# The last layer of a two-layer network on one core: values read in their PSUM bank, a projection step of their own, and another order of the turn

## What is computed

```python
# first attention: within one token, 16 heads of 16
Q, K, V = (x @ W.T).reshape(B, L, H, hd) for each of W_Q, W_K, W_V
sK = softmax(swapaxes(K, -1, -2), axis=-1)
tran_V = einsum('bldh,blhe->blde', sK, V)
x = layernorm(x + einsum('blhd,blde->blhe', softmax(Q, axis=-1), tran_V))
# second attention: layernorm, queries against 64 context rows under a mask, projection
x = layernorm(x + cross_attention(x, ctx, ...))
# feed-forward with ternary weights
h = silu(lin(x, w1)) * lin(x, w2)
h = gelu(lin(h, h1)); h = gelu(lin(h, h2))
x = layernorm(x + lin(h, w3))
```

## Time and profile before

| | |
|---|---|
| median of 3 runs | 1357.84 us (1355.26 to 1358.79) |
| profiled execution | 1360.66 us, its span from the first to the last instruction 1359.0 us |
| mean granted clock in the span | 0.908 |
| TensorE busy | 1072.8 us, 79% of the span |
| VectorE busy | 936.5 us, 69% |
| ScalarE busy | 592.4 us, 44% |
| GpSimd busy | 363.3 us, 27% |
| last layer | about 660 us to the end of the span |

### The profile page before, as it was taken

The page is one execution under the profiler, slowest core; times in us unless marked ns, Lnnn a source line. Parts: engine busy times, 40 slices in busy tenths (PEclk is TensorE's granted clock), DMA queues, the critical chain, the costliest instruction groups (busy, mean ns, idle before and its releaser), DMA issues. The chain is left out here.

```text
span 1359.0 us, 21042 instructions
## 1 busy us (share of the span) xinstructions
PE 1072.8 (79%) x6769; PEld 893.7 (66%) x6770; DVE 936.5 (69%) x1865; ACT 592.4 (44%) x1626; POOL 363.3 (27%) x493
## 2 busy tenths in 40 slices
PE   1599999675787599999425688888888888887887
PEld 1378888552376388889213577776777768776787
DVE  5689999766773012222399998989899898989321
ACT  0244444140361323323002466757665655757553
POOL 1001011100033200000500344626363443636232
PEclk9789999885895699999666799999999999999899
DMA  8015710000006656665270000000000000000000
GB/s 285 16 70 183 248 35 5 1 0 0 1 1 249 254 206 224 240 246 197 66 312 0 1 1 1 8 0 8 0 0 8 0 8 0 8 0 8 1 9 9
DMA packets 23974, 98.88 MB, mean 73 GB/s; under 512 B 3728, under 2 KB 15184, under 8 KB 17584
## 3 DMA queue, kind: packets, MB, share of 16 engines
q1 hardware_dynamic: 16080, 73.60, 14.7%
q10 hardware_dynamic: 5200, 17.37, 3.9%
q0 software_dynamic: 2640, 7.21, 1.5%
HBM read 87.96 MB, written 21.76 MB: 81 GB/s over the span
## 5 line engine op out<-in xcount | busy, mean ns | idle before, releaser
L2008 PE MATMUL bank<-n_hA_hi_reduced,ffn_h 128*128 128x256 f32 x512 | 125.1, 288 | 9.5 <-POOL n_hA_lo_reduced L1831 5.9
L2008 PE MATMUL bank<-n_hB_hi_reduced,ffn_h 128*128 128x256 f32 x512 | 128.7, 294 | 1.5 <-DVE n_hB_lo_reduced L2345 1.5
L2008 PE MATMUL bank<-n_hB_lo_reduced,ffn_h 128*128 128x256 f32 x512 | 124.2, 286 | 0.0
L2008 PE MATMUL bank<-n_hA_lo_reduced,ffn_h 128*128 128x256 f32 x512 | 122.3, 282 | 0.0
L1625 ACT ACTIVATE e_hT<-bank,e_b 128x128 f32<-128x128 f32 x184 | 52.6, 368 | 129.9 <-PE bank L1568 129.9
L2008 PEld LDWEIGHTS bank<-n_hA_hi_reduced,ffn_h 128*128 128x128 f32 x512 | 98.6, 193 | 11.2 <-POOL n_hA_lo_reduced L1831 10.5
L2008 PEld LDWEIGHTS bank<-n_hB_hi_reduced,ffn_h 128*128 128x128 f32 x512 | 100.7, 197 | 3.3 <-issue 3.3
L2259 DVE TENSOR_TENSOR d_prod<-d_qk,d_xT 128x512 f32<-128x512 f32 x128 | 102.1, 837 | 0.5
L2008 PEld LDWEIGHTS bank<-n_hB_lo_reduced,ffn_h 128*128 128x128 f32 x512 | 100.6, 197 | 1.7 <-issue 1.7
L2008 PEld LDWEIGHTS bank<-n_hA_lo_reduced,ffn_h 128*128 128x128 f32 x512 | 98.5, 192 | 0.1
L1650 DVE TENSOR_TENSOR e_y<-bank,e_b 128x256 f32<-128x256 f32 x23 | 9.8, 425 | 125.6 <-PE bank L1580 125.6
(11 more groups left out here) (347 smaller groups left out, 2690.9 us busy)
## 6 DMA issues: line engine op xcount, KB each, us to landing
e_w<-in_W SPq DMA_DIRECT2D x23, 1024.0 KB, 6.1
ffn_weights<-in_F ACTq DMA_DIRECT2D x2, 5632.0 KB, 21.0
e_piece<-ffn_weights SPq DMA_DIRECT2D x11, 1024.0 KB, 4.8
ffn_h<-ffn_weights SPq DMA_DIRECT2D x2, 4096.0 KB, 18.8
ffn_w<-ffn_weights SPq DMA_DIRECT2D x3, 1024.0 KB, 8.3
expert_rows<-zero ACTq DMA_DIRECT2D x1, 2944.0 KB, 10.6
e_xs<-expert_rows SPq DMA_DIRECT2D x23, 128.0 KB, 4.7
expert_out<-e_y POOLq DMA_DIRECT2D x23, 128.0 KB, 2.0
```

The lines of the kernel that those rows point to most:

```text
L2008: last = nc.tensor.matmul(F[f % 2][:, 0:PAIR], weight(w[:, k, f * P:(f + 1) * P], fast), operand(src[part][1][:, k, :], fast), start=(c == ...
```

## The change

The values stay in bank_v. `contexts` reads them there (`values`), `v_copied` and `vs` are gone, and a semaphore `v_read` tells TensorE when the fourth quarter is done. The projection of the values is a step of its own, `projected_v`, with its own semaphore `v_done`; `xn_copied`, which overwrites xT, waits for it. The turned x3 goes to the second half of bank_o instead of bank_v; so `turned_x3` waits for x3_copied of the tile before and for `out_summed` of the tile three before, and `summed` waits until the x3 of two tiles on is copied. The lists of all four engines are put in another order, and GpSimd's first two powers stand behind 4 and 8 gathers instead of 6 and 12. The arithmetic is the same. Lines of context are cut, and the indentation is shortened.

```diff
--- before.py
+++ after.py
@@ -1729,15 +1729,15 @@
 xn, r = x3, m.r
-vs = [t[:, :, :].rearrange("p k (e h) -> p (k e) h", h=H) for t in xT]
 T = late("d_T", [P, DH, DH], F32)[:, :, :]
...
 bank_o, bank_t, F = m.banks[4], m.banks[5], m.banks[6:8]
+values = bank_v[:, 0:D].rearrange("p (e h) -> p e h", h=H)
 gathered = [sem(f"d_gathered{n}") for n in range(3)]
-names = ("x_var", "x_pow", "x3", "x3_turned", "x3T", "qkv_done", "v_copied", "pre", "exp", "attn_var", "attn_pow",
+names = ("x_var", "x_pow", "x3", "x3_turned", "x3T", "qkv_done", "v_done", "v_read", "pre", "exp", "attn_var", "attn_pow",
  "xn", "xn_turned", "xnT", "score_done", "max", "sexp", "prob", "prob_turned", "probT", "out_done",
@@ -1851,39 +1851,38 @@
         tile(x_powered, n, 0)
+    pair(lower_parts, n - 3, 1, 2, 8)
+    tile(out_powered, n - 2, 1)
+    row_of(added, n - 3, 0)
     tile(attn_powered, n - 1, 0)
...
         x_powered(2, 1, 0)
-    pair(gated_product, n - 2, 0, 2)
+    tile(x5_kept, n - 2, 1)
+    row_of(added, n - 3, 1)
+    pair(gated_product, n - 2, 0, 4)
     pair(gate_lower, n - 2, 0, 1)
-    pair(gated_product, n - 2, 2, 4)
+    pair(gated_product, n - 2, 4, 6)
     pair(gate_lower, n - 2, 1, 2)
-    pair(gated_product, n - 2, 4, 5)
-    pair(gate_lower, n - 2, 2, 3)
-    pair(gated_product, n - 2, 5, 8)
-    pair(gate_lower, n - 2, 3, 8)
-    row_of(added, n - 3, 1)
+    pair(gated_product, n - 2, 6, 8)
+    pair(gate_lower, n - 2, 2, 8)
     row_of(y_powered, n - 3, 0)
-    pair(lower_parts, n - 2, 0, 0, 2)
     row_of(y_powered, n - 3, 1)
-    pair(lower_parts, n - 2, 0, 2, 5)
-    tile(attn_powered, n - 1, 1)
+    pair(lower_parts, n - 2, 0, 0, 3)
     if not (isinstance(n, int) and n == 0):
         tile(x_powered, n, 1)
-    pair(lower_parts, n - 2, 0, 5, 8)
+    tile(attn_powered, n - 1, 1)
     tile(out_powered, n - 1, 0)
+    pair(lower_parts, n - 2, 0, 3, 4)
     tile(x5_kept, n - 1, 0)
-    pair(lower_parts, n - 2, 1, 0, 8)
-    tile(out_powered, n - 1, 1)
-    tile(x5_kept, n - 1, 1)
-    row_of(added, n - 2, 0)
+    pair(lower_parts, n - 2, 0, 4, 8)
+    pair(lower_parts, n - 2, 1, 0, 2)
...
 for t in range(TB):
-    if t == 3:
+    if t == 2:
         x_powered(0, 0, 0)
-    elif t == 6:
+    elif t == 4:
         x_powered(1, 0, 1)
@@ -1905,20 +1904,28 @@
     pe.wait_ge(q["x3"], k + 1)
-    after("v_copied", k)
+    after("x3T", k)
+    after("out_var", k - 2)
     for c in range(KD):
-        last = nc.tensor.transpose(bank_v[:, D + c * P:D + (c + 1) * P], x3[b][:, c * P:(c + 1) * P],
+        last = nc.tensor.transpose(bank_o[:, D + c * P:D + (c + 1) * P], x3[b][:, c * P:(c + 1) * P],
                                    m.ident[:, :])
...
     after("pre", k)
-    for lo, hi, to in ((0, 2 * D, bank_qk), (2 * D, 3 * D, bank_v)):
-        for c in range(KD):
-            last = nc.tensor.matmul(to[:, 0:hi - lo], xT[b][:, c, :], m.wqkv1[:, c, lo:hi],
-                                    start=(c == 0), stop=(c == KD - 1))
+    for c in range(KD):
+        last = nc.tensor.matmul(bank_qk[:, 0:2 * D], xT[b][:, c, :], m.wqkv1[:, c, 0:2 * D],
+                                start=(c == 0), stop=(c == KD - 1))
     last.then_inc(q["qkv_done"], 1)
+def projected_v(k, i, b):
+    pe.wait_ge(q["x3T"], k + 1)
+    after("v_read", k)
+    for c in range(KD):
+        last = nc.tensor.matmul(bank_v[:, 0:D], xT[b][:, c, :], m.wqkv1[:, c, 2 * D:3 * D],
+                                start=(c == 0), stop=(c == KD - 1))
+    last.then_inc(q["v_done"], 1)
@@ -1951,6 +1958,7 @@
     after("out_var", k)
+    pe.wait_ge(q["x3T"], min(k + 3, NT) if isinstance(k, int) else k + 3)
     for c in range(KF):
@@ -2024,27 +2032,32 @@
     tile(qkv, n, 0)
+    tile(projected_v, n, 0)
     pair(hidden, n - 2, 0, 0, 2, fast)
     tile(turned_probs, n - 1, 0)
-    pair(hidden, n - 2, 0, 2, 7, fast)
+    pair(hidden, n - 2, 0, 2, 5, fast)
     tile(summed, n - 1, 0)
+    pair(hidden, n - 2, 0, 5, 7, fast)
     tile(turned_xn, n - 1, 1)
     pair(hidden, n - 2, 0, 7, 8, fast)
+    tile(scores, n - 1, 1)
+    pair(hidden, n - 2, 1, 0, 1, fast)
     tile(turned_x3, n, 1)
-    tile(scores, n - 1, 1)
-    pair(hidden, n - 2, 1, 0, 3, fast)
+    pair(hidden, n - 2, 1, 1, 4, fast)
     tile(turned_x5, n - 1, 0)
-    pair(hidden, n - 2, 1, 3, 5, fast)
+    pair(hidden, n - 2, 1, 4, 5, fast)
     tile(qkv, n, 1)
+    pair(hidden, n - 2, 1, 5, 6, fast)
+    tile(projected_v, n, 1)
     tile(turned_probs, n - 1, 1)
-    pair(hidden, n - 2, 1, 5, 8, fast)
+    pair(hidden, n - 2, 1, 6, 8, fast)
     tile(summed, n - 1, 1)
     row_of(final, n - 2, 0, fast)
+    tile(turned_x5, n - 1, 1)
     row_of(final, n - 2, 1, fast)
-    tile(turned_x5, n - 1, 1)
-    pair(first, n - 1, 0, 4, fast)
+    pair(first, n - 1, 0, 2, fast)
     tile(turned_xn, n, 0)
-    pair(first, n - 1, 4, 8, fast)
+    pair(first, n - 1, 2, 8, fast)
     tile(scores, n, 0)
@@ -2077,13 +2090,8 @@
         act.wait_ge(q["score_done"], k - 1)
-    nc.scalar.activation(xT[b][:, :, :].rearrange("p k n -> p (k n)"), bank_v[:, D:2 * D],
+    nc.scalar.activation(xT[b][:, :, :].rearrange("p k n -> p (k n)"), bank_o[:, D:2 * D],
                          ACT.Copy).then_inc(q["x3T"], 1)
-def v_copied(k, i, b):
-    act.wait_ge(q["qkv_done"], k + 1)
-    nc.scalar.activation(vs[b][:, :, :].rearrange("p a b -> p (a b)"), bank_v[:, 0:D],
-                         ACT.Copy).then_inc(q["v_copied"], 1)
@@ -2091,6 +2099,7 @@
     act.wait_ge(q["xn_turned"], k + 1)
+    act.wait_ge(q["v_done"], k + 1)
     for c in range(KD):
@@ -2147,36 +2156,34 @@
     tile(x3_copied, n, 0)
-    pair(gate_upper, n - 2, 7, 8)
+    pair(gate_upper, n - 2, 6, 8)
     tile(score_exp, n - 1, 0)
-    pair(hidden, n - 2, 0, 0, 5)
+    pair(hidden, n - 2, 0, 0, 2)
     tile(probs_copied, n - 1, 0)
-    pair(hidden, n - 2, 0, 5, 7)
+    pair(hidden, n - 2, 0, 2, 6)
     tile(qk_exp, n, 0)
     tile(xn_copied, n - 1, 1)
-    pair(hidden, n - 2, 0, 7, 8)
-    tile(v_copied, n, 0)
-    pair(hidden, n - 2, 1, 0, 1)
+    pair(hidden, n - 2, 0, 6, 8)
     tile(x3_copied, n, 1)
-    pair(hidden, n - 2, 1, 1, 3)
+    pair(hidden, n - 2, 1, 0, 4)
     tile(score_exp, n - 1, 1)
-    pair(hidden, n - 2, 1, 3, 4)
+    pair(hidden, n - 2, 1, 4, 5)
     tile(x5_copied, n - 1, 0)
-    tile(v_copied, n, 1)
-    pair(hidden, n - 2, 1, 4, 6)
+    pair(hidden, n - 2, 1, 5, 6)
     tile(probs_copied, n - 1, 1)
-    pair(hidden, n - 2, 1, 6, 8)
+    pair(hidden, n - 2, 1, 6, 7)
+    tile(qk_exp, n, 1)
+    pair(hidden, n - 2, 1, 7, 8)
     tile(x5_copied, n - 1, 1)
-    tile(qk_exp, n, 1)
-    pair(first, n - 1, 0, 2)
+    pair(first, n - 1, 0, 4)
     pair(gate_upper, n - 1, 0, 1)
-    pair(first, n - 1, 2, 4)
-    pair(gate_upper, n - 1, 1, 2)
     pair(first, n - 1, 4, 6)
     tile(xn_copied, n, 0)
-    pair(gate_upper, n - 1, 2, 4)
-    pair(first, n - 1, 6, 8)
-    pair(gate_upper, n - 1, 4, 7)
+    pair(gate_upper, n - 1, 1, 2)
+    pair(first, n - 1, 6, 7)
+    pair(gate_upper, n - 1, 2, 3)
+    pair(first, n - 1, 7, 8)
+    pair(gate_upper, n - 1, 3, 6)
@@ -2253,12 +2260,14 @@
     kn = groups(qk[b][:, D:2 * D])
-    v.wait_ge(q["v_copied"], k + 1)
+    v.wait_ge(q["v_done"], k + 1)
     to = T.rearrange("p e d -> p d e")
...
              lambda at, n: V.tensor_tensor(part[n], spread(kn[:, at:at + TWO, :], 2, DH),
-                                           spread(vs[b][:, :, :], 1, TWO), ALU.mult),
+                                           spread(values, 1, TWO), ALU.mult),
              lambda at, n: V.tensor_reduce(to[:, at:at + TWO, :], part[n], AX.X, ALU.add))
+    if quarter == 3:
+        v.sem_inc(q["v_read"], 1)
@@ -2359,55 +2368,55 @@
     tile(x3_normed, n - 1, 1)
-    tile(out_summed, n - 2, 0)
     tile(softmaxes, n - 1, 0)
     tile(contexts, n - 1, 0, 0)
-    tile(x5_normed, n - 2, 0)
     tile(scores_max, n - 2, 1)
...
     tile(contexts, n - 1, 0, 3)
-    tile(probabilities, n - 2, 1)
     tile(attended, n - 1, 0, 0)
     tile(attended, n - 1, 0, 1)
-    tile(x5_split, n - 2, 0)
+    tile(probabilities, n - 2, 1)
     tile(attended, n - 1, 0, 2)
+    tile(prepared, n - 1, 1)
     tile(attended, n - 1, 0, 3)
     tile(out_summed, n - 2, 1)
-    tile(prepared, n - 1, 1)
+    tile(x5_split, n - 2, 0)
     tile(x5_normed, n - 2, 1)
+    tile(attention_summed, n - 1, 0)
+    tile(x5_split, n - 2, 1)
     if isinstance(n, int) and n == LAST + 3:
...
     row_of(sums_read, n - 3, 1)
-    tile(x5_split, n - 2, 1)
     if isinstance(n, int) and n == LAST + 2:
         last_gates()
-    tile(attention_summed, n - 1, 0)
-    row_of(y_moments, n - 3, 0)
     tile(softmaxes, n - 1, 1)
...
     tile(contexts, n - 1, 1, 0)
+    tile(x3_normed, n, 0)
     tile(contexts, n - 1, 1, 1)
     tile(contexts, n - 1, 1, 2)
-    tile(x3_normed, n, 0)
+    tile(contexts, n - 1, 1, 3)
     tile(scores_max, n - 1, 0)
-    tile(contexts, n - 1, 1, 3)
     tile(attended, n - 1, 1, 0)
+    row_of(y_moments, n - 3, 0)
+    tile(attended, n - 1, 1, 1)
```

(5 more changed lines are left out.)

## The result

| | us |
|---|---|
| kernel before, median of 5 runs beside the new one | 1355.76 (1355.26 to 1358.79) |
| new kernel, median of 5 runs | 1350.22 (1348.39 to 1351.41) |
| ratio, 95% interval | 0.9946 (0.9932 to 0.996) |
| profiled execution, its span | 1350.22, 1348.6 |

The new kernel is faster by 5.5 us. The profiled executions differ by 10.4, but 3.9 of that lies ahead of the changed layer, in identical code: its first gather is issued at 657.7 before and at 653.8 after. From the first gather to the end it is 701.3 before and 694.8 after, 6.5 us.

A forecast was written before the change was run, and what follows sets the result against it. No engine is full; a trip is a chain between engines, with TensorE setting it. Trips of 75.2 instead of 77.1 give -9.3 over five, the ends +1.9: -7.4 from 1357.84, about 1350.5 us; 8-in-10 range 1333 to 1365.

The forecast's parts named there:

- start +1.1: Layer's start: VectorE begins about 4 us sooner but gives it back; net +1.1 us to the first full trip.
- The sum of 7.4: TensorE's waits in one full trip, added over nine places: from 10.1 us down to 7.4.
- The 0.2 for more switches: TensorE in a full trip: three more switches between kinds of matmul cost 0.2 us.
- place 6: Wait ahead of turned probabilities, tile 0: 1.6 to 2.4 us, VectorE's path 9.8 against 7.4 of TensorE work.
- place 7: Wait ahead of the turn of xn tile 1: 0.5 to 0 us, VectorE arriving within 0.3 us of it.
- one fall a trip: Granted clock falls to 0.50 once in each full trip, costing 1.6 us, so a trip takes 75.2.
- Rival C: Clock falls behind both turned-probabilities waits every trip: 76.8 to 77.8 us a trip, 1358 to 1364 in all; chance 0.20.
- what I named as making me wrong: Full trips: xn tile 1's turn waits over 1 us, clock falls twice a trip, or VectorE idles under 3 us.
- rival B: Places 6 and 9, both turned-probabilities waits, under 2 us; clock never falls; trips 73 to 73.7, 1334 to 1342 us; chance 0.22.
- My lower bound: VectorE's context products: gain of 0 if the long broadcast reading of a bank collides with GpSimd all the same.
- rival D: Context products: GpSimd holds up a bank operand like the others; 77.8 us a trip, about 1368 in all; chance 0.05.
- No step waits on v_read for long: TensorE's projection of values stands some 10 us behind the previous tile's last context quarter, so no long wait.

The follow-up runs named there:

- the probabilities sooner: New kernel with VectorE's probabilities of tile 0 moved one attended quarter sooner in all trips; 1355.96 us, ratio 1.0009.
- filled versions: New kernel with unused matmuls ahead of turned probabilities: four at both tiles 1331.46 us, tile 1 only 1336.97, two at both 1334.17.
- the overfilled kernel: New kernel with eight unused matmuls added ahead of each turn of the probabilities; 1343.37 us, ratio 0.9923.
- without the 2.3 us wait: New kernel with tile 0's projection of values moved behind the turned probabilities in start trips 1 and 2; 1349.04 us, ratio 0.9943.

## Why the prediction was right, and which errors cancelled

The forecast was 1350.5, the measurement 1350.22; the median before it was 1355.76 rather than 1357.84, so the change won 5.5 where I had 7.4. That the two times agree within 0.3 us is luck. In the terms of the sum: five trips -9.3 forecast, -9.9 measured; start +1.1 and +3.2; last trip and end +0.8 and +0.2. The mean trip came out at 75.1 for a forecast of 75.2, by two errors that cancelled.

**The waits** were sized too high. A trip without a clock fall takes 72.5 to 72.7, not 73.6. Place by place, forecast and measured: final 0.45, 0.56; turn of x5 0.5, 0.1; first units with the turn of xn 1.3, 1.0; both turns of x3 0, 0; projection 0.7, 0.55; turned probabilities 2.4, 2.36 and 2.1, 2.13; turn of xn tile 1 0, 0. The sum of 7.4 is 6.7. The 0.2 for more switches can't be told from nothing: a trip without falls is 3.3 shorter, the waits 3.4. At place 6 the terms I listed for VectorE add up to 9.5, not 9.8; with 9.5 the wait would have been 2.1, and the 2.36 measured is nearer to the wrong sum. "Only just" at place 7 was right: a microsecond or two more on VectorE, as with the probabilities sooner, and it waits 2.36.

**The clock** was sized too low: I counted one fall a trip, and there are 1.6, at 1.5 each, 2.4 us for my 1.6. Rival C's mechanism, a fall behind both waits, holds in three trips of five, on a shorter trip; what I named as making me wrong, two falls a trip, came true in three trips of five. That these waits bring the falls of the new kernel is shown by its filled versions. Filling gives a trip without falls, as rival B had it, but at 72.5, not 73 to 73.7, and in 1331 us, not 1334 to 1342.

**VectorE's products** were right: 0.69 forecast, 0.681 measured, and 0.928 when only the operand's place is undone. The Trainium skill, VectorE: DVE Perf Modes, section "The TRN2 errata", has a bank source cost more than one in SBUF. The runs don't bear that out: 692 ns for both in the earlier trace rows, and beside a busy GpSimd the bank source was the cheaper by 0.25 us. My lower bound, a gain of nothing from it, and rival D are ruled out by the 681. I had called GpSimd's share, gates that end sooner, worth nothing more; with the values in SBUF TensorE waits 1.0 us a trip for these gates.

**What sets the trip.** That TensorE's chain sets it was the basis of the sum, and the overfilled kernel shows it for both turned probabilities. But I counted the two parts of the change as if each had its worth by itself. The removed wait on v_copied alone came back at the same place as a wait for the sums; in the new order, where out_summed stands at the end of VectorE's trip, it is gone. No run moved out_summed alone.

**The ends.** Nine table loads a trip are there. The last trip's wait for the gates is 2.62, forecast 3.3, and the trip is 0.9 shorter; the stretch behind it is 1.1 longer, so +0.2 for +0.8. The start was mis-sized, +3.2 for +1.1. "No step waits on v_read for long" is right for the full trips, where the projection of values waits 0.0, and wrong for the start, with 9.1, 2.3 and 9.1. The granted clock differs too, 0.77 in that stretch against 0.79 in the kernel before,

```profile
657.70:837.20 179.50, 109.59 (x531) 80.16 (x531) 155.65 (x293) 65.83 (x227) 54.65 (x64) 0.79 0.18 71
```

and filling, with 0.81, makes it 5.6 shorter. But the clock alone isn't it: with the probabilities in their old place the start has 0.79 and takes 182.9. What the start pays stays open. The old place of the probabilities doesn't shorten it; without the 2.3 us wait it takes 180.0, with the values in SBUF, where the projection never waits, 180.6, both at a clock of 0.79, and the medians can't tell 2 us.

## What to carry to other kernels

When an order of work gathers TensorE's scattered waits into a few longer ones, look at the granted clock of each trip before believing the sum: here 1.4 of 3.4 us won were given back, and 0.85 us of matmuls for nothing inside each of the two waits brought the ratio from 0.9946 to 0.9817. Such filling is no rule: in the old order it moved the falls to another wait and gained nothing. An operand kept in its PSUM bank can be worth more than the copy it saves, where another engine works on SBUF beside it; here most of it showed only in an order in which nothing waited for that bank. And undo each half of a two-part change alone: worths of 1.1 and nothing made 3.3.
